# Cross-attention of 16 batches on one core: special keys' K kept on chip, another order of the first loads, first row maxima on ACT's queue, an end in two chains

## The chip, the core and the metric

The kernel runs on one core of a Trainium2 chip. A core has a matrix engine (TensorE, PE in the rows, with PEld for its weight loads), a vector engine (VectorE, DVE), an activation engine (ScalarE, ACT), a general engine (GpSimd, POOL) and a queue engine (SyncE, SP) that here only issues DMAs. ACT and POOL can issue DMAs as well. The metric is device time in microseconds (us), the median of several runs. Before: 520.08 us, median of 3 runs (519.92 to 520.15).

## What is computed

```python
B, S, D, C = 16, 256, 320, 512        # batches, queries, model and context width
HEADS, NUM_IP, NUM_DUMMY = 20, 4, 4   # head width 16; 256 keys per batch
text, ip_h = ctx[:, :248], ctx[:, 248:]
q = split_heads(x @ w_q)
out_text = softmax(q @ split_heads(text @ w_k).T / 4) @ split_heads(text @ w_v)
mask = ip_mask(bbox)                  # 0 or -10000 per query and special key
out_ip = softmax(q @ split_heads(ip_h @ w_k_ip).T / 4 + mask) @ split_heads(ip_h @ w_v_ip)
out = (merge(out_text) + merge(out_ip)) @ w_out + b_out + x
```

248 of the 256 keys of a batch are text keys. The last 8 are the special keys; their K and V come from other weights, and they have a softmax of their own.

## The kernel before, in words

**Arithmetic.** Every projection is done with split operands: ACT writes the rounded upper part of a matrix (`..._hi`), DVE the rest (`..._lo`), and PE sums three products (helper `three`, L659 to L661). x, ctx and the weights are split that way, and so is each K and Q tile on its way out of PSUM (ACT L461, then DVE L562, both into `qk_out`).

**Tiles.** Two batches form a group. A group has ten tiles: three K tiles (128, 128 and 64 rows by 512 columns), four V tiles (128 by 320), three Q tiles (like K). A K tile is twelve matmuls, so there are 24 K tiles with 288 matmuls in all. SP stores K and Q tiles to DRAM (`k_parts`, `q_parts`) and V tiles to `v_rows`, and reads them back in another layout into `k_stack`, `q_stack` (L280, L274, L276) and `v_stage` (L296). The stacks hold, per pair of heads, the upper and lower parts, mask rows, and a row of negative maxima. The K of the special keys of all batches is made once, in `special()`, split into `ksp_parts`, and POOL writes it into the last 8 columns of every batch in `k_parts` with six DMAs (L399). `load_stack_k(0)` waits for these six (`ksp_stored`).

**Lone tiles.** Tiles 0 to 14 run before any attention work. Tiles of later groups are hosted: PE does one after every second pair of heads (`tile` in the PE batch loop). ACT and DVE give a tile's PSUM bank free when they have read it; tile 15, the first hosted one, goes into the bank of tile 14.

**A batch.** `batch(t)` has ten steps p, one per pair of heads. PE computes the key-major scores of batch t (`key_scores`, L757, into `score_t`), the query-major scores of batch t + 1 (`query_scores`, L702), the products with V (`values`, L772), and the output projection of batch t - 1 (`project_out`, L781, into `pj`). ACT takes exp of the key-major scores (L503) and empties `pv` (L495). DVE takes row maxima of the query-major scores (L571, L573), turns them (`turn`, L579), and turns and inverts the results (L612, L615, L620). POOL normalises (L421, L426). The maxima go to DRAM (`store_rows`, L251) and back into the stack as a row (`load_rows`, L256), in two halves per batch; `key_scores` of a half waits for them. Batch -1 only makes maxima for batch 0, with tiles 15 to 19. DVE's `finish` (L627) adds the residual and SP stores the output (L303).

**Order.** All orders are written out by hand, one program per engine. SP runs its DMAs strictly in program order: an issue whose semaphore is late holds up all behind it. The same holds for ACT and DVE.

## Time and profile before

| what | value |
|---|---|
| median of 3 runs | 520.08 us |
| profiled execution, its own time | 520.33 us |
| its span | 518.5 us |
| PE busy | 477.4 us (92%) |
| DVE busy | 380.7 us (73%) |
| ACT busy | 275.3 us (53%) |
| POOL busy | 151.6 us (29%) |
| DMA moved | 101.80 MB, mean 196 GB/s |

The span is that of the recorded instructions; 1.83 us lie around it. Times below count from the start of the span. A row of a timeline gives start, duration, engine, line, operation, what is written from what is read, and in brackets the engine's idle time ahead of it with what ended it. Matmul durations overlap, so what one costs is the distance from start to start. A duration of a DMA on SPq is the issue alone, not the transfer.

### The profile page before, as it was taken

The page shows a single profiled execution, that of the slowest core. Times are in us where ns is not written, and L with a number is a line of the kernel's source. Part 1 is how long each engine was busy: PE and PEld are TensorE (multiplying, and loading weights), DVE is VectorE, ACT ScalarE, POOL GpSimd, SP SyncE. Part 2 cuts the span into 40 slices and gives each one's busy share as a digit, 9 for nine tenths or more (in the row PEclk, how much of TensorE's full clock was granted, in tenths as well). Part 3 has the DMA queues.
Part 4 walks back from the last instruction along what each step waited for, and adds up shares of the span by engine and source line. Part 5 has one row for each costly group of instructions (what it writes and reads, how often), then busy time and mean ns, then how long its engine had stood idle before and what let it go on. Part 6 is the DMA issues. An engine that isn't in the chain of part 4 may idle for free.

```text
span 518.5 us, 11114 instructions
## 1 busy us (share of the span) xinstructions
PE 477.4 (92%) x4306; PEld 321.8 (62%) x4306; DVE 380.7 (73%) x687; ACT 275.3 (53%) x355; POOL 151.6 (29%) x242
## 2 busy tenths in 40 slices
PE   2999669999999999999999999999999999898895
PEld 2787536576666766676666766676666765554542
DVE  3833476877877787877877787877887779999732
ACT  3643124465655656465655655465555546666670
POOL 4570000423313131414313141413304131543331
PEclk9999797999999999999999999999999999999998
DMA  8999975837593856837593856937584736273011
GB/s 272 303 232 290 351 255 163 261 107 231 150 326 100 282 179 166 278 114 246 149 332 96 268 194 170 274 111 246 148 284 149 256 123 210 86 252 84 9 53 51
DMA packets 96438, 101.80 MB, mean 196 GB/s; under 512 B 16881, under 2 KB 83489, under 8 KB 96385
## 3 DMA queue, kind: packets, MB, share of 16 engines
q1 hardware_dynamic: 95392, 98.92, 61.1%
q0 software_dynamic: 992, 2.17, 1.8%
q8 instruction: 34, 0.56, 0.4%
q14 instruction: 20, 0.16, 0.1%
HBM read 67.87 MB, written 33.23 MB: 195 GB/s over the span
## 4 chain that ended last, share of the span: by engine, by line
issue 54%; POOL 23%; PE 9%; DMA 5%; DVE 4%; SPq 2%; ACT 1%; POOLq 0%; ACTq 0%
POOL o_turned L421 10%; POOL o_all L426 6%; POOL x_all L413 5%; POOL v_cur L408 2%; DMA v_rows<-v_out 1%; PE score_q L659 1%; DMA q_parts<-qk_out 1%; PE pv L772 1%; PE score_q L660 1%; PE score_q L661 1%; DMA max_rows<-row_buf 1%; DMA probs<-in_wk 1%; PE pj L781 1%; DMA raw<-in_ctxT 1%; SPq L247 1%
## 5 line engine op out<-in xcount | busy, mean ns | idle before, releaser
L571 DVE TENSOR_REDUCE max_cols<-score_q 128x4 fp32r<-128x992 f32 x155 | 183.0, 1181 | 85.3 <-PE score_q L702 84.8
L503 ACT ACTIVATE probs<-score_t 128x1024 f32<-128x1024 f32 x160 | 163.4, 1021 | 145.5 <-PE score_t L757 145.5
L772 PE MATMUL pv<-probs,v_cur 128*32 128x256 f32 x1920 | 120.2, 383 | 0.6 <-ACT probs L503 0.6
L421 POOL TENSOR_TENSOR o_turned<-o_turned,inv_cols 128x256 f32<-128x256 f32 x80 | 54.4, 679 | 157.0 <-DVE inv_cols L615 157.0
L772 PEld LDWEIGHTS pv<-probs,v_cur 128*32 128x32 f32 x1920 | 54.3, 109 | 39.1 <-issue 1.0
L781 PE MATMUL pj<-wo_sb,o_all 128*128 128x320 f32 x192 | 70.4, 477 | 8.9 <-DVE out_sb L627 4.8
L413 POOL TENSOR_TENSOR x_all<-x_all,bias_sb 128x640 f32<-128x640 f32 x16 | 25.2, 1575 | 150.0 <-DMA x_all<-in_x 150.0
L612 DVE STREAM_TRANSPOSE o_turned<-o_all 128x512 f32<-128x512 f32 x80 | 55.9, 698 | 11.9 <-ACT o_all L495 11.9
L757 PEld LDWEIGHTS score_t<-q_stack,k_stack 64*128 64x128 f32 x440 | 33.0, 185 | 48.5 <-issue 34.8
L495 ACT ACTIVATE o_all<-pv 128x512 f32<-128x512 f32 x80 | 47.8, 598 | 28.5 <-PE pv L772 28.5
L757 PE MATMUL score_t<-q_stack,k_stack 64*128 64x256 f32 x440 | 55.7, 331 | 7.6 <-ACT probs L503 6.9
L702 PE MATMUL score_q<-k_stack,q_stack 64*128 64x256 f32 x420 | 43.5, 285 | 7.7 <-DMA q_stack<-aux_rows 5.3
L781 PEld LDWEIGHTS pj<-wo_sb,o_all 128*128 128x128 f32 x192 | 31.9, 193 | 25.9 <-DVE out_sb L627 8.4
L659 PE MATMUL score_q<-wv_hl,c_hi 128*128 128x320 f32 x112 | 40.2, 359 | 0.0
L702 PEld LDWEIGHTS score_q<-k_stack,q_stack 64*128 64x128 f32 x420 | 32.9, 188 | 9.9 <-issue 7.2
L426 POOL TENSOR_TENSOR o_all<-o_turned 128x128 f32<-128x128 f32 x80 | 36.6, 457 | 6.3
L661 PE MATMUL score_q<-wv_hl,c_hi 128*128 128x320 f32 x112 | 35.3, 315 | 0.0
L660 PE MATMUL score_q<-wv_hl,c_lo 128*128 128x320 f32 x112 | 35.2, 315 | 0.0
L659 PE MATMUL score_q<-c_hi,wk_hl 128*128 128x512 f32 (+1 forms) x72 | 32.6, 452 | 0.0
L661 PE MATMUL score_q<-c_lo,wk_hl 128*128 128x512 f32 (+1 forms) x72 | 29.1, 404 | 0.0
L660 PE MATMUL score_q<-c_hi,wk_hl 128*128 128x512 f32 (+1 forms) x72 | 29.0, 403 | 0.0
L562 DVE TENSOR_TENSOR qk_out<-score_q,qk_out 128x512 fp32r<-128x512 f32 (+1 forms) x40 | 27.4, 685 | 1.7 <-ACT qk_out L461 1.3
(151 smaller groups left out, 656.0 us busy)
## 6 DMA issues: line engine op xcount, KB each, us to landing
k_stack<-k_parts SPq DMA_DIRECT2D x33, 320.0 KB, 4.9
q_stack<-q_parts SPq DMA_DIRECT2D x33, 320.0 KB, 5.7
q_parts<-qk_out SPq DMA_DIRECT2D x32, 256.0 KB, 4.7
k_parts<-qk_out SPq DMA_DIRECT2D x32, 248.0 KB, 5.3
raw<-in_ctxT SPq DMA_DIRECT2D x14, 512.0 KB, 4.4
v_rows<-v_out SPq DMA_DIRECT2D x32, 160.0 KB, 4.7
v_stage<-v_rows SPq DMA_DIRECT2D x16, 320.0 KB, 6.2
x_all<-in_x SPq DMA_DIRECT2D x16, 320.0 KB, 6.1
```

Source lines behind the costliest of these rows:

```text
L421: pool.tensor_tensor(out, out, inv_cols[:, n % SLOTS, :].unsqueeze(2).broadcast_to([P, 2 * S // 32, DH]), ALU.mult).then_inc(scaled, 1)
L426: pool.tensor_tensor(o_norm_t[:, k // 2, :, half:half + DH], out[:, 0:S // 32, :], out[:, S // 32:, :], ALU.add).then_inc(o_added, 1)
L503: nc.scalar.activation(probs[:, slot(t % 2, p), :], score_t[:, :], ACT.Exp, scale=SCALE)\
L571: nc.vector.tensor_reduce(out=max_cols[:, h, :, at:at + 4:2].rearrange("p t e -> p e t"), in_=both[:, :, :, 0:TEXT], op=ALU.max, axis=AX.X ...
L612: nc.vector.transpose(turned_blocks(n), o_raw[:, n % SLOTS, :].rearrange("p (j n) -> p j n", n=32))\
L659: mm(out, w_hi, x_hi_, start=start, stop=False)
L660: mm(out, w_lo, x_hi_, start=False, stop=False)
L661: return mm(out, w_hi, x_lo_, start=False, stop=stop)
L702: last = mm(score_bank(b, p, e)[:, tile * KEYS:(tile + 1) * KEYS], q_cols(b % 3, p, e, tile * P, P), k_cols(b % 3, p, e, 0, KEYS), start=T ...
L757: last = mm(score_t[:, 512 * e + S * tile:512 * e + S * tile + S], k_cols(b % 3, p, e, tile * P, P), q_cols(b % 3, p, e, 0, S), start=True ...
L772: last = mm(pv[32 * t:32 * t + 32, at:at + S], values_of(u, kind, 4 * k + t), probs[:, slot(u, 2 * k + t // 2), a:a + S], start=kind != 1, ...
L781: last = mm(pj[:, 0:D], o_norm[:, b % 2, c, t * P:t * P + P], wo_sb[:, c, :], start=c == 0, stop=c == OC - 1)
```

## The change

The K columns of the special keys no longer go through DRAM on their own. `ksp_parts` has its own memory and stays. A K tile is now computed, split and read out in its text columns only (2 x 248 instead of 512, helper `columns`). Then DVE copies the special columns of the group from `ksp_parts` into `qk_out` (`fill`), and SP stores whole rows after `k_filled`. For tiles 0 to 2 the fill comes after `special()`; POOL's six DMAs and `ksp_stored` are gone.

SP's first loads and stores are reordered. The V tiles 3 and 4 and the c loads of group 1 go ahead of the stores of K tiles 0 to 2, `load_stack_k(0)` ahead of the Q stores, `load_x(1)` behind `load_stack_q(0)`, `load_small` into batch 0. ACT and DVE split x of group 1 later. The first half of the first row maxima is stored and loaded by ACT. `turn` stands directly behind its last maxima.

In the last batch the odd steps of `key_scores` use a second bank, and `project_out` of the last batch runs both row tiles side by side in two banks, each with its own store.

The diff, cut to its core:

```diff
@@ tiles and banks @@
+        ksp_parts = sb("ksp_parts", [P, 2, XC, P], f32r)
-        ksp_parts = o_turned[:, 0:2 * XC * P].bitcast(f32r).rearrange("p (s m n) -> p s m n", s=2, m=XC)
+        def key_bank(b, p):
+            return score_q[:, 0:1024] if b == B - 1 and p % 2 else score_t[:, :]
+        def out_bank(b, t):
+            return score_t[:, 0:D] if b == B - 1 and t else pj[:, 0:D]
+        def columns(row, j):
+            return row if j >= 3 else row.rearrange("p (b n) -> p b n", b=GB)[:, :, 0:TEXT]
@@ SP @@
-                sp.wait_ge(lo_done, 6 * g + j + 1)
+                if j >= 3:
+                    sp.wait_ge(lo_done, 6 * g + j + 1)
+                else:
+                    sp.wait_ge(k_filled, 3 * g + j + 1)
                 for s in range(2):
...
+                    parts = q_parts if j >= 3 else k_parts
+                    sp.dma_start(parts[s, m * P:m * P + r, g * GT:(g + 1) * GT], src[:, s, :])\
+                        .then_inc(qk_stored[ring], 16)
...
-            lone(0, 5)
+            lone(3, 5)
             for h in range(2):
                 load_c(1, h)
+            lone(0, 3)
             lone(5, 7)
-            load_x(1)
+            load_stack_k(0)
             lone(7, 10)
-            sp.wait_ge(ksp_stored, 96)
-            load_stack_k(0)
             sp.wait_ge(aux_stored, 96)
             load_stack_q(0)
-            lone(10, 12)
+            load_x(1)
+            lone(10, 14)
             sp.wait_ge(sp_stored, 16)
-            load_small()
-            lone(12, 14)
...
-                if host and t % 2 and g + 1 < GROUPS:
+                if host and t > 0 and t % 2 and g + 1 < GROUPS:
                     load_c(g + 1, 0)
                 if ahead:
                     need(sp, st_ready, PAIRS * t)
                     load_stack_k(t + 2)
+                if t == -1:
+                    load_c(g + 1, 0)
...
-                if next_:
+                if next_ and t >= 0:
                     store_rows(t + 1, 0)
...
-                if next_:
+                if next_ and t >= 0:
                     load_rows(t + 1, 0)
@@ POOL @@
-            for m, r in enumerate(MT_ROWS):
-                pool.wait_ge(ksp_lo, m + 1)
-                for s in range(2):
-                    pool.dma_start(k_parts[s, m * P:m * P + r, :].rearrange("p (b n) -> p b n", b=B)[:, :, TEXT:KEYS],
-                                   ksp_parts[0:r, s, m, :].rearrange("p (b n) -> p b n", b=B).bitcast(f32))\
-                        .then_inc(ksp_stored, 16)
@@ ACT @@
-            tile(10)
+            for n in range(10, 14):
+                tile(n)
             split_x(1)
-            for n in range(11, 14):
-                tile(n)
+            def store_first_rows():
+                act.wait_ge(rows_turned, 1)
+                act.dma_start(max_rows[0].rearrange("r (t i n) -> i r t n", t=2, i=4),
+                              row_buf[:, 0, :].rearrange("p (t n) -> p t n", t=2)).then_inc(first_stored, 16)
+            def load_first_rows():
+                act.wait_ge(first_stored, 16)
...
+                    if t == -1 and p == 6:
+                        store_first_rows()
+                    if t == -1 and p == 8:
+                        load_first_rows()
@@ DVE @@
+                if j < 3 and g:
+                    fill(g, j)
+            def fill(g, m):
+                r, w = MT_ROWS[m], GB * NSP
+                nc.vector.tensor_copy(
+                    qk_out[0:r, m, :, :].rearrange("p s (b n) -> p s b n", b=GB)[:, :, :, TEXT:KEYS],
+                    ksp_parts[0:r, :, m, g * w:(g + 1) * w].rearrange("p s (b n) -> p s b n", b=GB))\
+                    .then_inc(k_filled, 1)
...
-            tile(10)
+            for n in range(10, 13):
+                tile(n)
             split_x(1)
-            tile(11)
-            tile(12)
@@ PE @@
-                need(pe, exp_done, PAIRS * b + p)
+                if b < B - 1 or p == 0:
+                    need(pe, exp_done, PAIRS * b + p)
+                elif p == 1:
+                    pe.wait_ge(max_done, PAIRS * B)
+                else:
+                    pe.wait_ge(exp_done, PAIRS * b + p - 1)
...
+LAST_OUT = {3: [(0, 0), (1, 0), (0, 1), (1, 1)], 5: [(0, 2), (1, 2)]}
```

SP's queue from the stores of K tile 2 (before) to the mask row of the first stack. Before:

```order
L247 DMA k_parts<-qk_out 64x2x248 x2
L233 DMA v_rows<-v_out 128x320 x2
L217 DMA raw<-in_ctxT 128x2x512
L217 DMA o_all<-in_ctxT 128x2x512
L233 DMA v_rows<-v_out 128x320 x2
L224 DMA o_all<-in_xT 128x2x512
L226 DMA o_all<-in_xT 64x512 x2
L242 DMA q_parts<-qk_out 128x512 x4
L242 DMA q_parts<-qk_out 64x512 x2
L280 DMA k_stack<-k_parts 32x10x256 x3
L274 DMA q_stack<-q_parts 32x10x256 x3
L276 DMA q_stack<-aux_rows 32x10x256
```

Now, from the c loads to the x load:

```order
L223 DMA raw<-in_ctxT 128x2x512
L223 DMA o_all<-in_ctxT 128x2x512
L251 DMA k_parts<-qk_out 128x512 x4
L251 DMA k_parts<-qk_out 64x512 x2
L239 DMA v_rows<-v_out 128x320 x2
L284 DMA k_stack<-k_parts 32x10x256 x3
L251 DMA q_parts<-qk_out 128x512 x4
L251 DMA q_parts<-qk_out 64x512 x2
L278 DMA q_stack<-q_parts 32x10x256 x3
L280 DMA q_stack<-aux_rows 32x10x256
L230 DMA o_all<-in_xT 128x2x512
L232 DMA o_all<-in_xT 64x512 x2
```

The K stores moved behind the c loads, the K reads moved ahead of the Q stores, and the x load moved from ahead of the Q stores to behind the mask row.

ACT's queue from tile 10 to the first exp. Before (v_out rows are V tiles 13 to 16, x_hi the split of x of group 1, c_hi the two halves of c of group 2):

```order
L461 ACTIVATE qk_out<-pj 128x512
L445 ACTIVATE x_hi<-o_all 128x1536
L461 ACTIVATE qk_out<-pv 128x512
L461 ACTIVATE qk_out<-score_t 64x512
L456 ACTIVATE v_out<-score_t 128x320
L454 ACTIVATE v_out<-score_q,text_mask 128x320
L456 ACTIVATE v_out<-score_q 128x320
L454 ACTIVATE v_out<-score_q,text_mask 128x320
L441 ACTIVATE c_hi<-raw 128x1024
L461 ACTIVATE qk_out<-score_q 128x512 x2
L441 ACTIVATE c_hi<-raw 128x1024
L503 ACTIVATE probs<-score_t 128x1024
```

Now, from tile 13:

```order
L459 ACTIVATE v_out<-score_t 128x320
L448 ACTIVATE x_hi<-o_all 128x1536
L457 ACTIVATE v_out<-score_q,text_mask 128x320
L459 ACTIVATE v_out<-score_q 128x320
L457 ACTIVATE v_out<-score_q,text_mask 128x320
L444 ACTIVATE c_hi<-raw 128x1024
L464 ACTIVATE qk_out<-score_q 128x512
L496 DMA max_rows<-row_buf 4x64x32
L464 ACTIVATE qk_out<-score_q 128x512
L444 ACTIVATE c_hi<-raw 128x1024
L501 DMA q_stack<-max_rows 4x5x256
L515 ACTIVATE probs<-score_t 128x1024
```

The split of x moved behind tiles 11 to 13 and stands directly ahead of tile 14; two DMAs of the row maxima joined the queue, the second behind the second half of c.

PE at the very end, from the last key-major scores (with waits). Before:

```order
L757 MATMUL score_t<-q_stack,k_stack 128x256 [waits exp_done]
L757 MATMUL score_t<-q_stack,k_stack 128x256 x3
L781 MATMUL pj<-wo_sb,o_all 128x320
L772 MATMUL pv<-probs,v_cur 32x256 [waits exp_done,o_evac]
L772 MATMUL pv<-probs,v_cur 32x256 x11
L781 MATMUL pj<-wo_sb,o_all 128x320 [waits out_done,o_ready]
L781 MATMUL pj<-wo_sb,o_all 128x320 [waits o_ready] x2
L781 MATMUL pj<-wo_sb,o_all 128x320 [waits out_done]
L781 MATMUL pj<-wo_sb,o_all 128x320 x2
```

Now:

```order
L790 MATMUL score_q<-q_stack,k_stack 128x256 [waits exp_done]
L790 MATMUL score_q<-q_stack,k_stack 128x256 x3
L814 MATMUL pj<-wo_sb,o_all 128x320
L805 MATMUL pv<-probs,v_cur 32x256 [waits exp_done,o_evac]
L805 MATMUL pv<-probs,v_cur 32x256 x11
L814 MATMUL pj<-wo_sb,o_all 128x320 [waits out_done,o_ready]
L814 MATMUL score_t<-wo_sb,o_all 128x320 [waits out_done]
L814 MATMUL pj<-wo_sb,o_all 128x320 [waits o_ready]
L814 MATMUL score_t<-wo_sb,o_all 128x320
L814 MATMUL pj<-wo_sb,o_all 128x320 [waits o_ready]
L814 MATMUL score_t<-wo_sb,o_all 128x320
```

The three matmuls of the second row tile moved from behind the first tile's `finish` to between the first tile's own, in a bank of their own, and the last key scores are in `score_q`.

## Rows read from the trace of the kernel before

**Rows 1.** Page, part 1: busy time of each engine.
```profile
PE 477.4 (92%) x4306; PEld 321.8 (62%) x4306; DVE 380.7 (73%) x687; ACT 275.3 (53%) x355; POOL 151.6 (29%) x242
```

**Rows 2.** Matmul groups, 100 to 430 us: busy, mean ns, idle before, what ended it.
```profile
L781 PE MATMUL pj<-wo_sb,o_all 128*128 128x320 f32 x132 | 47.3, 467 | 6.1 <-DVE out_sb L627 4.2 <-DVE o_all L620 1.9
```

**Rows 3.** Stretches: length, PE, PEld, DVE, ACT, POOL busy, clock, DMA share, GB/s.
```profile
34.00:36.00 2.00, 2.00 (x10) 1.64 (x9) 1.18 (x2) 2.00 (x3) 2.00 (x3) 1.00 0.97 108
```

**Rows 4.** SP's issues, timeline; SPq L247 and L242 merge six issues with waits between.
```profile
15.61 7.98 SPq L247 DMA_DIRECT2D k_parts<-qk_out  x6
...
37.81 6.15 SPq L242 DMA_DIRECT2D q_parts<-qk_out  x6
44.22 1.98 SPq L280 DMA_DIRECT2D k_stack<-k_parts  x3
47.38 1.90 SPq L274 DMA_DIRECT2D q_stack<-q_parts  x3
```

**Rows 5.** Four K stores issued from 50.0 to 51.8 us: issue to landing.
```profile
DMA to landing us min/median/max: 5.2/5.9/6.7
```

**Rows 6.** DVE's timeline, the start.
```profile
28.27 0.28 DVE L597 TENSOR_TENSOR o_turned<-score_q,o_turned 64x128 fp32r<-64x128 f32 x1 [0.42 <-ACT o_turned L478]
...
47.52 1.22 DVE L551 TENSOR_TENSOR x_lo<-o_all,x_hi 128x1024 fp32r<-128x1024 f32 x1 [0.69 <-ACT x_hi L445]
48.78 0.69 DVE L553 TENSOR_TENSOR x_hi<-o_all,x_hi 64x512 fp32r<-64x512 f32 x1
...
68.71 1.27 DVE L547 TENSOR_TENSOR c_lo<-raw,c_hi 128x1024 fp32r<-128x1024 f32 x1
```

**Rows 7.** PE's timeline, the start; the times in brackets are idle time.
```profile
55.95 0.80 PE L702 MATMUL score_q<-k_stack,q_stack 64*128 64x256 f32 x4 [5.32 <-DMA q_stack<-aux_rows]
...
57.10 0.63 PE L659 MATMUL score_q<-wv_hl,c_hi 128*128 128x320 f32 x1
...
60.60 0.70 PE L702 MATMUL score_q<-k_stack,q_stack 64*128 64x256 f32 x4
...
80.42 0.79 PE L659 MATMUL score_q<-c_hi,wk_hl 128*128 128x512 f32 x1
```

**Rows 8.** The chain that ended last, 44 to 80 us: start, duration, what.
```profile
46.01 1.49 ACT x_hi L445
...
66.31 4.75 DMA max_rows<-row_buf
...
71.69 4.28 DMA raw<-in_ctxT
...
76.00 1.06 ACT c_hi L441
```

**Rows 9.** PE's timeline: where a 512-column tile and two 320-column tiles start.
```profile
17.51 0.40 PE L659 MATMUL score_t<-c_hi,wk_hl 128*64 128x512 f32 x1
...
20.27 0.30 PE L659 MATMUL score_t<-wv_hl,c_hi 128*128 128x320 f32 x1
...
22.03 0.31 PE L659 MATMUL score_q<-wv_hl,c_hi 128*128 128x320 f32 x1
```

**Rows 10.** Timeline of all engines: the last batch and the end.
```profile
495.08 1.50 PE L772 MATMUL pv<-probs,v_cur 128*32 128x256 f32 x24
...
498.21 0.50 PE L757 MATMUL score_t<-q_stack,k_stack 64*128 64x256 f32 x4 [0.46 <-ACT probs L503]
...
498.65 1.50 PE L772 MATMUL pv<-probs,v_cur 128*32 128x256 f32 x24
...
510.40 0.81 PE L781 MATMUL pj<-wo_sb,o_all 128*128 128x320 f32 x2 [0.61 <-DVE o_all L620]
511.24 0.49 DVE L627 TENSOR_TENSOR out_sb<-pj,x_all 128x320 f32<-128x320 f32 x1 [0.90 <-PE pj L781]
...
515.81 0.38 SPq L303 DMA_DIRECT2D out<-out_sb  x1
```

**Rows 11.** The last output store, issued at 515.81 us: issue to landing.
```profile
DMA to landing us min/median/max: 2.3/2.3/2.3
```

More of the change, by code:

```diff
@@ L360, in _ @@
                 batch(t)
-            for b in (B - 2, B - 1):
-                store_out(b)
-            sp.wait_ge(out_stored, 16 * B)
+            store_out(B - 2)
+            for t in range(OT):
+                sp.wait_ge(out_done, OT * (B - 1) + t + 1)
+                at = (B - 1) * S + t * P
+                sp.dma_start(out[at:at + P, :], out_sb[:, t, :]).then_inc(out_stored, 16)
+            sp.wait_ge(out_stored, 16 * (B - 1 + OT))
         @block.gpsimd
@@ L460, in tile @@
                     need(act, qk_stored[j % 3], 32 * (2 * g + j // 3))
-                    nc.scalar.activation(qk_out[0:r, j % 3, 0, :], tile_bank(n)[0:r, :], ACT.Copy).then_inc(hi_done, 1)
+                    nc.scalar.activation(columns(qk_out[0:r, j % 3, 0, :], j), columns(tile_bank(n)[0:r, :], j),
+                                         ACT.Copy).then_inc(hi_done, 1)
             high(wk_hl[:, 0], wk_raw, ld["wk"], 16)
@@ L577, in turn @@
                 dve.wait_ge(max_done, PAIRS * b + HALF * (h + 1))
-                need(dve, rows_stored, 16 * (2 * b + h - 1))
+                if b == 1 and h == 0:
+                    dve.wait_ge(first_stored, 16)
+                need(dve, rows_stored, 16 * (2 * b + h - 2))
                 nc.vector.transpose(row_buf[:, h, :].rearrange("p (t n) -> p t n", t=2),
@@ L626, in finish @@
                     dve.wait_ge(biased, b + 1)
-                nc.vector.tensor_tensor(out_sb[:, t, :], pj[:, 0:D], x_res[:, b % 2, t, :], ALU.add)\
+                nc.vector.tensor_tensor(out_sb[:, t, :], out_bank(b, t), x_res[:, b % 2, t, :], ALU.add)\
                     .then_inc(out_done, 1)
@@ L633, in batch @@
                         maxima(t + 1, p)
+                    if p % HALF == HALF - 1 and there(t + 1):
+                        turn(t + 1, p // HALF)
                     n = tile_due(t, p) if t >= 0 or p else None
@@ L649, in batch @@
                         split_x(g)
-                    if p % HALF == HALF - 1 and there(t + 1):
-                        turn(t + 1, p // HALF)
             for t in range(-1, B + 1):
@@ L666, in k_tile @@
                         pe.wait_ge(c_split, 2 * g + c // 2 + 1)
-                    last = three(out[0:r, :], wk_hl[:, 0, c, cols], wk_hl[:, 1, c, cols], c_hi[:, c, :],
-                                 c_lo[:, c, :], c == 0, c == CC - 1)
+                    last = three(columns(out[0:r, :], m), wk_hl[:, 0, c, cols], wk_hl[:, 1, c, cols],
+                                 columns(c_hi[:, c, :], m), columns(c_lo[:, c, :], m), c == 0, c == CC - 1)
                 last.then_inc(tile_ready, 1)
@@ L753, in key_scores @@
                     pe.wait_ge(rows_loaded[p // HALF], 16 * (b + 1))
-                need(pe, exp_done, PAIRS * b + p)
+                if b < B - 1 or p == 0:
[4 more added lines that the diff above has]
+                    pe.wait_ge(exp_done, PAIRS * b + p - 1)
+                both = key_bank(b, p)
                 for tile in range(2):
                     for e in range(2):
-                        last = mm(score_t[:, 512 * e + S * tile:512 * e + S * tile + S],
+                        last = mm(both[:, 512 * e + S * tile:512 * e + S * tile + S],
                                   k_cols(b % 3, p, e, tile * P, P), q_cols(b % 3, p, e, 0, S), start=True, stop=True)
@@ L779, in project_out @@
                 if c == 0:
-                    need(pe, out_done, OT * b + t)
-                last = mm(pj[:, 0:D], o_norm[:, b % 2, c, t * P:t * P + P], wo_sb[:, c, :],
+                    need(pe, out_done, OT * b + (t if b < B - 1 else 0))
+                last = mm(out_bank(b, t), o_norm[:, b % 2, c, t * P:t * P + P], wo_sb[:, c, :],
                           start=c == 0, stop=c == OC - 1)
@@ L785, in batch @@
             def batch(t):
+                if t == 1:
+                    pe.wait_ge(ld["small"], 32)
                 if t == 0:
-                    pe.wait_ge(ld["small"], 32)
                     for back in range(1, 6):
@@ L798, in batch @@
                             values(t + off, k)
-                    for m, k in OUT.get(p, ()):
+                    for m, k in (OUT if t < B else LAST_OUT).get(p, ()):
                         if there(t - 1):
```

29 lines of the change are left out of this document (14 added, 15 removed).

## The prediction

> **What bounds the kernel now.** I read the page's busy shares first: PE is busy for 92% of the span [rows 1], so a microsecond counts only where PE is shortened or stops waiting. The matmul groups of 100 to 430 us then show where it waits inside the regular batches: one group has idle time ahead of it, 6.1 us in 330 [rows 2]. There PE is the bound, and DVE, ACT, POOL or DMA work that changes is free. What is left is the start and the end. At the start PE idles 5.32 us ahead of the first query scores, until the mask row (aux_rows) of the first stack has landed [rows 7]; SP's issues and the chain of waits say what holds that up and what follows [rows 4, 8]. At the end the timeline shows PE, ACT and DVE taking turns [rows 10].
>
> **Regular batches.** A 512-column tile starts 2.76 us ahead of the next tile and a 320-column one 1.76 us, twelve matmuls each [rows 9]: 0.230 and 0.147 us a matmul, 0.43 ns a column. Sixteen columns fewer are 6.9 ns. 18 of the 24 K tiles are hosted, 216 matmuls, so 1.5 us go. The six lone tiles lose 0.5 us, which only lengthens the wait for the stack. That the operand is now two pieces of 248 columns is in no row; I take it as free, with the price in a rival below. DVE gains 24 small copies, near 0.2 us each (the nearest row is the 64x128 subtraction, 0.28 [rows 6]). They stand behind the subtraction that frees the PSUM bank, so PE doesn't wait for them; only SP's K store does. **-1.5 us**, between -1.5 and 0.
>
> **Start, the first stack.** What goes are POOL's six DMAs of 32-byte pieces; in 34 to 36 us the DMA engines were 97% busy for only 108 GB/s [rows 3]. What is added is a wait: the stores of K tiles 0 to 2 were issued from 15.6 to 23.6 us [rows 4] and now need the special keys' K, whose last lower part is done at 28.55 [rows 6]. With the copy they are issued until about 30.4. They land behind c and the POOL loads; the landings of 5.2 to 6.7 us in a full queue [rows 5] make it 35.6 to 37.1, I take 36. On SP the reads of K stand behind that wait, and behind them the Q stores: 36 + 2.0 for three reads [rows 4] + six issues at 0.65 (a third of 1.98) = 41.9, against 43.96 before (37.81 + 6.15). The Q stack reads were issued 3.4 us behind that end (47.38), so now at 45.3. From there to PE's start it took 8.57 us (55.95 - 47.38), so PE starts at about 53.9, 2.1 us earlier. The bounds are 0.5 (K stores land last) and 4 us (the queue is empty).
>
> **Start, what comes next.** The x load of group 1 was ahead of the Q stores; now it stands behind the mask row. Four issues of 0.65 put it at 47.9 to 49.8. The K stores that stood in that place took 5.2 to 6.7 us [rows 5], so x is in at about 55.2. On ACT the split of x (1.49, [rows 8]) now stands directly ahead of V tile 14, and tile 15 needs that tile's PSUM bank: 55.2 + 1.5 + 0.45 for the eviction = 57.2. Before, tile 15 started at 57.10 [rows 7]. On DVE the two subtractions, 1.22 + 0.69 [rows 6], stand ahead of the first maxima: these start at 58.6, and the next query scores, which need them, at 59.8. Before, these started at 60.60 and were held by tile 15, since PE ran at half its clock (tile 15 took 3.5 us where a V tile takes 1.76 [rows 7, 9]). So the 2.1 us are given back: behind tile 15 both kernels stand at the same point. I expect half clock there again, since PE has idled longer in pieces.
>
> **Start, the first row maxima.** Before, their store took 4.75 us to land, SP stood still for it, and the second half of c for group 2 went out behind it, at 71.69 [rows 8]. DVE had made room for it at 69.98 (68.71 + 1.27, [rows 6]). Now nothing blocks SP there, and c goes out 1.7 us earlier: 70.0, landing after 4.28 at 74.3, split by ACT until 75.4. But the load of the maxima stands behind that split on ACT. Issued at 75.4 it needs the 2.3 us of a small transfer without a queue [rows 11] (4.75 in a full one, [rows 8]): 77.7. Key scores of batch 0, exp (1.0), second key and query scores: the first hosted K tile starts near 79.9, against 80.42 [rows 7]. **-0.5 us** for the whole start. Its bounds are -4 (x and c land in time for PE to run through) and +3 (x lands 2 us late and half clock lasts longer).
>
> Here a rule of the Trainium skill speaks against the move. DMA: Bandwidth & Descriptors, section Issuing engines are not separate DMA queues, says that issuing from another engine saves only the issue time on the sequencer. By that rule the gain would be some 1.1 us of SP's two issues. The chain of waits of this case shows more: what SP loses is its standstill. By the rule alone the start would come out 0.6 us slower than I say.
>
> The small weights now load in batch 0, behind the residual; POOL's first normalisation waits for them about 1.3 us longer (two issues). Its first results are needed at the end of batch 0: nothing.
>
> **The last batch.** From one group of products with V to the next it takes 3.57 us (495.08 to 498.65). Of that 3.13 run over ACT's eviction and the odd step's exp to the even key scores at 498.21, and 0.44 are these key scores [rows 10]. With a second bank the key scores come earlier, and the period is 3.13, or PE's own work where two thirds of a projection stand in it (1.50 for the products, 2 x 0.44, and twice 0.54 = 3.46, less the overlap of their ends, about 3.4; 0.54 is an estimate from the 0.81 of a third's two matmuls, whose ends overlap what follows). The first group comes 0.44 earlier, the next three periods save 0.2, 0.44 and 0.2, the last 0.1. **-1.4 us**, between -0.6 and -2.
>
> **The end.** Before, the last third of the first row tile starts at 510.40 and its residual add at 511.24; only then the second row tile is multiplied, at half clock, and its store is issued at 515.81 [rows 10]. Now the second tile's third follows directly, 0.54 us later at full clock: result at 511.78, add until 512.3, store at 512.3. **-3.5 us**; -3.0 if PE is at half clock. The first tile's store is issued half a microsecond earlier and lies beside it. POOL, which makes the last values, keeps its distance: its operations depend on the same evictions.
>
> **Sum.** -1.5 - 0.5 - 1.4 - 3.5 = -6.9. The profiled execution took 520.33 us (span 518.5 and 1.83 around it), so 513.4 for it; the median lies 0.25 below, which gives 513.2.
>
> **Rivals.** (1) The start works: K stores land by 35, x by 53.5, and tile 15 follows the first query scores at once. Then the 2 us of the first wait stay, and half clock goes with them (1.7 us for tile 15): 509.8. For it: the small pieces are gone from the busiest stretch. Against: x goes out behind two more sets of transfers than before. (2) The start loses: x lands at 57 to 58 behind the stack, tile 15 starts at 59.5, and the load of the maxima adds to it: 515.8. For it: the landings of 6.7 us. (3) The end gives less: exp stays the bound in the last batch, because ACT's evictions wait as before, and only the two chains help: 514.6. (4) Slower: the two-piece operand costs PE time at every piece. It decides at 288 matmuls x 19 ns = 5.4 us, which eats all other gains; at 30 ns each it is 8.6 us and gives 523.3. The slowest rate seen, half clock, would be 0.2 us each. Against it: the score matmuls write and read blocks of 256 columns at full pace. (5) The change doesn't remove the wait: the mask row lands when it did, since the Q reads wait for the Q stores all the same. That is inside the forecast, whose start gives next to nothing.
>
> **Chances.** Forecast 0.45, its own range 512 to 514.3; (1) 0.2, (2) 0.2, (3) 0.1, (4) 0.03; 0.02 for no change through several small losses. The range leaves out (4), the zero and the outer edges of (1) and (2): 509.8 to 516.6. A measurement of this kernel can tell about 0.2%, 1.0 us, from no change. Faster 0.95, same 0.02, slower 0.03.
>
> **What would show it.** PE's idle time ahead of the first query scores: 3 to 4 us instead of 5.32. ACT's split of x: start at 55.2; the first hosted V tile right behind V tile 14's eviction. The load of the row maxima: issued behind ACT's second c split, near 75.4, with PE waiting for it at the first key scores. Matmuls of K tiles: start to start 0.223 us at full clock. Last batch: 3.13 to 3.4 us between groups of L772's kind. The last two stores of the output: about half a microsecond apart. I am wrong if K tile matmuls don't get shorter, if PE starts the first hosted K tile over 2 us off 79.9, or if the last two stores are over 1 us apart.

## The result: slower, not faster

The changed kernel took **523.13 us** (median of 13 runs, 521.37 to 527.66) against 520.08 of the kernel before (13 runs measured beside it, 517.17 to 521.85). The ratio is 1.0079 with a 95% interval of 1.0054 to 1.0105. The forecast was 513.2, its range ended at 516.6. So 10 us are missing, and the sign is wrong.

Lines of the profile's page of the kernel after, parts 1 and 5 (columns as in [rows 1]; in part 5 busy us and mean ns, then the idle time ahead of the group and what ended it):

```profile
span 521.7 us, 11133 instructions
PE 476.3 (91%) x4306; PEld 322.5 (62%) x4306; DVE 391.0 (75%) x711; ACT 275.2 (53%) x355; POOL 148.7 (29%) x236
...
L814 PE MATMUL pj<-wo_sb,o_all 128*128 128x320 f32 x186 | 66.9, 468 | 10.5 <-DVE out_sb L654 6.4
```

PE's work shrank by 1.1 us [rows 1], yet the span grew by 3.2. DVE has 10.3 us more: half of it (5.5) is the 24 small copies, nearly all of the rest one instruction that got longer, below. The matmul groups of 100 to 430 us show where PE stands still now. [Rows 2] had 6.1 us in one group; now it is 9.2 there and 2.5 ahead of the query scores (1.6 of it in the group shown):

```profile
L814 PE MATMUL pj<-wo_sb,o_all 128*128 128x320 f32 x130 | 46.5, 467 | 9.2 <-DVE out_sb L654 6.4 <-DVE o_all L647 2.8
...
L729 PE MATMUL score_q<-k_stack,q_stack 64*128 64x256 f32 x288 | 29.7, 283 | 1.6 <-DVE max_cols L597 1.5
```

To place the loss I compare the start of ACT's exp in both kernels. There is one for each step, ten for each batch, and I take the tenth of every batch as its end: the length of batch 2 runs from the last exp of batch 1 to the last exp of batch 2. Batch 2 (hosting, even) begins and ends so, first before, then after (where the last row is the end of batch 3):

```profile
133.77 1.02 ACT L503 ACTIVATE probs<-score_t 128x1024 f32<-128x1024 f32 x1
...
163.67 1.02 ACT L503 ACTIVATE probs<-score_t 128x1024 f32<-128x1024 f32 x1
```
```profile
135.23 1.02 ACT L515 ACTIVATE probs<-score_t 128x1024 f32<-128x1024 f32 x1
...
166.50 1.02 ACT L515 ACTIVATE probs<-score_t 128x1024 f32<-128x1024 f32 x1
...
194.98 1.02 ACT L515 ACTIVATE probs<-score_t 128x1024 f32<-128x1024 f32 x1
```

Batch 2 takes 29.90 us before and 31.27 after. Batch 3, odd, takes 28.48 in both (166.50 to 194.98; before 163.67 to 192.15). The same holds for batches 4, 6, 8 and 10. So the account by stages is: start +1.5 us (the lag at batch 2: 135.23 - 133.77), the ten batches 2 to 11 +6.6 together (all of it in the five even ones), last batches and end -4.9. The sum is +3.2. The end did what was forecast. The regular batches and the start did not.

The +1.5 flatters the start. The first exp comes 3.64 us later (80.60 against 76.96), and batch 0 gives 2.16 of that back (first exp to first exp 29.26 against 31.42). Some 1.2 of it is a long instruction that the kernel before has in batch 0 and the kernel after happens not to have, below.

### The profile page after: what moved, and what is told of

Read it like the earlier page. It is cut to its first block, busy times and chain, and to the rows that moved or that the text cites. A ratio compares the mean times of both kernels' runs of the same rounds, so it can differ in the third digit from the quotient of the medians.

```text
span 521.7 us, 11133 instructions
## 1 busy us (share of the span) xinstructions
PE 476.3 (91%) x4306; PEld 322.5 (62%) x4306; DVE 391.0 (75%) x711; ACT 275.2 (53%) x355; POOL 148.7 (29%) x236
## 4 chain that ended last, share of the span: by engine, by line
PE 62%; DVE 15%; issue 9%; DMA 7%; SPq 3%; POOL 2%; ACT 2%; POOLq 0%; DVEq 0%; ACTq 0%
PE pv L805 13%; PE score_t L790 9%; PE pj L814 9%; PE score_q L686 8%; PE score_q L688 7%; PE score_q L687 7%; PE score_q L729 5%; DVE max_cols L595 5%; DVE x_hi L569 2%; DVE qk_out L578 1%; DVE x_lo L567 1%; SPq L251 1%; DVE out_sb L654 1%; DMA o_all<-in_xT 1%; DMA k_parts<-qk_out 1%
## 5 line engine op out<-in xcount | busy, mean ns | idle before, releaser
L515 ACT ACTIVATE probs<-score_t 128x1024 f32<-128x1024 f32 x155 | 158.4, 1022 | 150.8 <-PE score_t L790 150.7
L424 POOL TENSOR_TENSOR o_turned<-o_turned,inv_cols 128x256 f32<-128x256 f32 x80 | 56.3, 704 | 171.8 <-DVE inv_cols L642 171.8
L814 PE MATMUL pj<-wo_sb,o_all 128*128 128x320 f32 x186 | 66.9, 468 | 10.5 <-DVE out_sb L654 6.4
L416 POOL TENSOR_TENSOR x_all<-x_all,bias_sb 128x640 f32<-128x640 f32 x16 | 27.1, 1696 | 137.7 <-DMA x_all<-in_x 110.1
L507 ACT ACTIVATE o_all<-pv 128x512 f32<-128x512 f32 x80 | 47.9, 599 | 32.2 <-PE pv L805 32.2
L790 PEld LDWEIGHTS score_t<-q_stack,k_stack 64*128 64x128 f32 x420 | 31.6, 186 | 45.3 <-issue 37.8
L790 PE MATMUL score_t<-q_stack,k_stack 64*128 64x256 f32 x420 | 53.2, 331 | 6.8 <-DMA q_stack<-max_rows 3.7
L814 PEld LDWEIGHTS pj<-wo_sb,o_all 128*128 128x128 f32 x186 | 30.0, 188 | 26.4 <-DVE out_sb L654 9.5
L686 PE MATMUL score_q<-c_hi,wk_hl 128*128 128x496 f32 (+1 forms) x72 | 32.1, 445 | 0.0
L687 PE MATMUL score_q<-c_hi,wk_hl 128*128 128x496 f32 (+1 forms) x72 | 28.8, 400 | 0.0
L688 PE MATMUL score_q<-c_lo,wk_hl 128*128 128x496 f32 (+1 forms) x72 | 28.7, 399 | 0.0
L597 DVE TENSOR_REDUCE max_cols<-score_q 128x4 fp32r<-128x32 f32 x155 | 28.0, 181 | 0.0
```

Source lines behind the costliest of these rows:

```text
L424: pool.tensor_tensor(out, out, inv_cols[:, n % SLOTS, :].unsqueeze(2).broadcast_to([P, 2 * S // 32, DH]), ALU.mult).then_inc(scaled, 1)
L507: nc.scalar.activation(o_raw[:, n % SLOTS, :], pv[:, :], ACT.Copy).then_inc(o_evac, 1)
L515: nc.scalar.activation(probs[:, slot(t % 2, p), :], key_bank(t, p), ACT.Exp, scale=SCALE)\
L686: mm(out, w_hi, x_hi_, start=start, stop=False)
L687: mm(out, w_lo, x_hi_, start=False, stop=False)
L688: return mm(out, w_hi, x_lo_, start=False, stop=stop)
```

## What is different in an even batch

DVE's timeline in step 4 of batch 2, before, then after:

```profile
151.06 1.18 DVE L551 TENSOR_TENSOR x_lo<-raw,x_hi 128x1024 fp32r<-128x1024 f32 x1
152.28 0.69 DVE L553 TENSOR_TENSOR x_hi<-raw,x_hi 64x512 fp32r<-64x512 f32 x1
153.00 0.25 DVE L579 STREAM_TRANSPOSE row_buf<-max_cols 128x64 f32<-128x64 f32 x1
```
```profile
151.54 0.24 DVE L605 STREAM_TRANSPOSE row_buf<-max_cols 128x64 f32<-128x64 f32 x1
...
152.27 0.16 DVE L585 CAST qk_out<-ksp_parts 128x32 fp32r<-128x32 f32 x1
...
152.71 1.18 DVE L567 TENSOR_TENSOR x_lo<-raw,x_hi 128x1024 fp32r<-128x1024 f32 x1
153.92 1.95 DVE L569 TENSOR_TENSOR x_hi<-raw,x_hi 64x512 fp32r<-64x512 f32 x1
```

The same subtraction of 64x512 takes 0.69 us before and 1.95 after. POOL's timeline of the same stretch, before and after:

```profile
152.94 1.57 POOL L413 TENSOR_TENSOR x_all<-x_all,bias_sb 128x640 f32<-128x640 f32 x1 [10.92 <-DMA x_all<-in_x]
```
```profile
153.44 1.88 POOL L416 TENSOR_TENSOR x_all<-x_all,bias_sb 128x640 f32<-128x640 f32 x1 [9.83 <-DMA x_all<-in_x]
155.28 1.07 POOL L424 TENSOR_TENSOR o_turned<-o_turned,inv_cols 128x256 f32<-128x256 f32 x1
```

POOL adds the bias to the residual as soon as the residual has landed. Before, it begins 0.03 us ahead of the end of x_hi. After, it is asked for during x_lo, stands until that ends (1.88 instead of 1.57 us), and then x_hi, which also reads two operands from SBUF, stands until POOL's addition ends at 155.32; it ends at 155.87, 0.55 us later. POOL's next operation in turn takes 1.07 us, where it takes 0.62 before, since x_hi now stands in its way. It looks as if one of the two engines has to wait for the end of the other's whole operation. (Spans on POOL are rough in this profile; the reading rests on DVE's own row.) How this reaches PE is seen in its idle times in batch 2, before and then after:

```profile
151.19 0.81 PE L781 MATMUL pj<-wo_sb,o_all 128*128 128x320 f32 x2 [0.34 <-DVE o_all L620]
...
157.91 1.34 PE L781 MATMUL pj<-wo_sb,o_all 128*128 128x320 f32 x4 [0.36 <-DVE out_sb L627]
```
```profile
152.83 0.81 PE L814 MATMUL pj<-wo_sb,o_all 128*128 128x320 f32 x2 [0.56 <-DVE o_all L647]
...
157.24 0.51 PE L729 MATMUL score_q<-k_stack,q_stack 64*128 64x256 f32 x4 [0.45 <-DVE max_cols L597]
...
160.71 1.34 PE L814 MATMUL pj<-wo_sb,o_all 128*128 128x320 f32 x4 [0.81 <-DVE out_sb L654]
```

Behind x_hi, PE stands 0.45 us for the row maxima and 0.45 more for the output addition. The 0.22 more for o_all come ahead of x_hi, where the early turn and the new copy stand on DVE.

All instances of x_lo and x_hi from 90 to 400 us (minimum/median/maximum in ns), after and then before:

```profile
L567 DVE TENSOR_TENSOR x_lo<-raw,x_hi x6: 1180/1182/1214, 96.7 to 391.8; 128x1024 fp32r<-128x1024 f32 x6
L569 DVE TENSOR_TENSOR x_hi<-raw,x_hi x6: 690/1946/2066, 98.0 to 393.0; 64x512 fp32r<-64x512 f32 x6
```
```profile
L553 DVE TENSOR_TENSOR x_hi<-raw,x_hi x6: 689/690/1950, 95.2 to 386.0; 64x512 fp32r<-64x512 f32 x6
```

The kernel before has one of them too, in batch 0: its 1950. A mean hides it, the maximum shows it.

The Trainium skill has the rule: SBUF — State Buffer, section Who interferes with whom, says that a DVE tensor_tensor with both inputs in SBUF contends with GpSimd's reads. It calls the ports that the two share an exclusive lock, and says of DVE's two-port modes that the one issued first keeps them for its whole instruction while the other blocks fully. If that goes for tensor_tensor too, x_hi ends at POOL's end plus about its own time; the trace agrees (155.32 + 0.55, where x_hi alone takes 0.69).

## Experiments

Theory A: this exclusion costs the even batches 1.2 us each. Theory B: the K tiles' two-piece operand or the new copies do. For the start: the late x costs it, or the late first stack does. The first four kernels below ran on one chip, the next four (before_end, before_end_late, after_old_late, after_x_first) on a second, after_k3 and the three of x_first_k3 on a third. Each group had the kernel before beside it (519.82, 520.82 and 519.32 us); the ratios are to that, and kernels of different chips are best compared by them.

**POOL waits for the split of x (after_gate, before_gate).**

```diff
                 pool.wait_ge(xr_loaded[u], 8 * (b - u) + 16)
+                if hosted(b) and b % 2 == 0:
+                    pool.wait_ge(x_tail, (b + 4) // 2 + 1)
```

> The kernel after with one wait more: in the even hosted batches POOL's addition of bias to the residual starts only when DVE's second lower part of x is written. Theory A (DVE and POOL exclude each other on operations that read both operands from SBUF): the subtraction with output x_hi, 1.94 to 2.07 us in five batches, takes 0.69 in all of them, each of these batches gets about 1.3 us shorter, and the time falls by 6 to 6.7 us, from 523.1 to about 516.8. Theory B (the K tiles' two-piece operand and the added DVE copies cost the time): nothing changes, 523.1, or a little more, since POOL starts its normalisation up to 1 us later.

> The kernel before with the same wait on POOL. Its trace has one long x_hi subtraction (1.95 us, in batch 0) and margins of 0.6 to 1.7 us in the others. Theory A: 1.2 us go with the one of batch 0, 520.1 to about 518.9, and the spread between executions gets smaller, since no collision is left to chance. Theory B: no change, 520.1.

Measured: after_gate 519.58 us, ratio to before 0.9992 (0.9965 to 1.0020); before_gate 518.04, ratio 0.9958 (0.9929 to 0.9987). In both x_hi takes 0.69 us in every batch. Before_gate does what A said for the time, with 1.8 instead of 1.2 us by the medians and 1.2 in batch 0 of its trace. It didn't do what I expected for the spread: its 12 runs lie between 515.88 and 520.84, the 29 of the kernel before between 516.59 and 524.10. After_gate wins 3.5 us by the medians and 4.5 by the ratios, where 6 to 6.7 were expected. In its profiled execution the five even batches give back 4.4 us, and the start is 2.0 us later before the edit can act; such differences of 1 to 2 us in the start came between executions more than once, and I have no cause for them. Batch 2 fell from 31.27 to 30.58 only: POOL's results now come later, and the third small copy of the batch still meets POOL's copy of V, as in the kernel after (0.43 us, 0.16 alone). So B falls, but a wait is a poor cure.

**The turn of the maxima alone (after_turn_old, before_turn_new).** In after_turn_old the turn goes back behind the split, in before_turn_new it comes ahead. The edit of before_turn_new (that of after_turn_old is its reverse):

```diff
                     if there(t + 1):
                         maxima(t + 1, p)
+                    if p % HALF == HALF - 1 and there(t + 1):
+                        turn(t + 1, p // HALF)
...
-                    if p % HALF == HALF - 1 and there(t + 1):
-                        turn(t + 1, p // HALF)
```

> The kernel after with DVE's turn of the row maxima back at the end of its step, behind the split of x. The split moves 0.25 us forward. Theory A with the phase as cause: POOL's addition still starts ahead of x_hi by 0.1 to 0.6 us in four of the five batches, so only one or two collisions go: 1.3 to 2.7 us less, about 521. Rival (the place of the turn by itself makes the loss): all of it goes, 516.5 to 517.

> The kernel before with only the turn of the maxima moved ahead of the hosted tile. The split of x moves back by 0.25 us, the margin to POOL's addition shrinks from 0.6 or more to 0.35 or more. Theory A with the phase as cause: no new collision, 520 within 1 us. Rival (the place of the turn by itself): five collisions of 1.3 us, 526.5.

Measured: after_turn_old 517.59 us, ratio 0.9956 (0.9929 to 0.9983); before_turn_new 526.09 (four runs), ratio 1.0102 (1.0059 to 1.0144). Here the rival's numbers came out, not mine. The mechanism was still the collision. In after_turn_old every x_hi takes 0.69 us. In before_turn_new, where nothing but this line is changed, one of the two is long in each of the five batches (four times x_hi, once x_lo):

```profile
L551 DVE TENSOR_TENSOR x_lo<-raw,x_hi x5: 1180/1184/2487, 151.3 to 389.9; 128x1024 fp32r<-128x1024 f32 x5
L553 DVE TENSOR_TENSOR x_hi<-raw,x_hi x5: 999/1950/1959, 152.5 to 391.1; 64x512 fp32r<-64x512 f32 x5
```

I had moved only DVE's side of the race by 0.25 us. The turn also releases SP's store of the maxima, and all of SP's later issues stand behind that store. SP's timeline from the last store of batch 3 to the residual of batch 4, before and before_turn_new:

```profile
194.94 0.54 SPq L251 DMA_DIRECT2D max_rows<-row_buf  x1
...
205.22 0.47 SPq L300 DMA_DIRECT2D x_all<-in_x  x1
```
```profile
194.17 0.54 SPq L251 DMA_DIRECT2D max_rows<-row_buf  x1
...
205.28 0.47 SPq L300 DMA_DIRECT2D x_all<-in_x  x1
```

By batch 4 before_turn_new lags by 1.09 us in exp, yet it stores the maxima 0.77 us earlier and issues the residual at the same time: 1 us earlier in its own step. In batch 2, where there is no lag yet, the residual goes out 0.42 us earlier (146.06 against 146.48). So the split comes later and the residual earlier. Both push towards the collision.

**POOL's addition moved away (before_end_late, after_old_late, after_x_first, after_k3).** Before_end takes only the change's end over into the kernel before (key_bank, out_bank, the waits of the last batch's key scores, LAST_OUT and the two stores):

```diff
-                    for m, k in OUT.get(p, ()):
+                    for m, k in (OUT if t < B else LAST_OUT).get(p, ()):
...
-            for b in (B - 2, B - 1):
-                store_out(b)
+            store_out(B - 2)
+            for t in range(OT):
+                sp.wait_ge(out_done, OT * (B - 1) + t + 1)
...
```

Before_end_late also moves the addition:

```diff
...
+                late = hosted(b) and b % 2 == 0
+                if not late:
+                    add_bias()
                 for k in range(QUADS):
+                    if k == 2 and late:
+                        add_bias()
```

> The kernel before with only the end of the change: a second bank for the odd key scores of the last batch, its output as two chains in two banks, two stores. Theory A (the end works and lies on its own): the last exp 0.7 us earlier and 4.0 us less from there to the last store, as the trace of after shows, 520.1 to about 515.4. Rival (part of the 4 us comes from the later phase of the kernel after): 517 or more.

> The same, and in the even hosted batches POOL's addition of bias to the residual moved behind its second group of products (k = 1), where DVE has no subtraction from SBUF. Theory A (exclusion of DVE and POOL): the long x_hi of batch 0 goes, 1.3 us less than before_end, 514.1, and five executions in a row lie closer together. Theory B (the long x_hi is hidden or due to something else): the same as before_end.

Measured: before_end 515.82 us (514.60 to 516.81), ratio 0.9905 (0.9875 to 0.9936); before_end_late 514.24 (513.95 to 514.49), ratio 0.9878 (0.9849 to 0.9906). The end is worth 5 us on its own. The collision of batch 0 costs 1.6 by the medians and 1.2 at the first exp of batch 1 in the traces (its x_hi: 1.95, then 0.69), and the spread shrinks from 2.2 to 0.5 us, over six and five runs. That the order of two engines, set by when a DMA lands, is behind a part of the spread of the kernel before is possible but not shown: before_gate still ranged over 5.0 us, and no collisions were counted run by run.

> The kernel after with the turn of the maxima at its old place and POOL's addition moved as in before_end_late. Theory A: x_hi takes 0.69 us in every batch, and POOL doesn't wait as it did in after_gate: no batch is longer than in the kernel before. Start 1.5 to 2.5 us later than before, last batch and end 4.7 earlier, K tiles up to 0.8 us: 516.5 to 517.5.

(The kernel is after_turn_old with POOL's addition moved as in before_end_late.) Measured: 520.87 us, ratio 1.0013 (0.9993 to 1.0033), 3.4 above the upper end of what I expected; by the ratios 3.0 more than after_turn_old. I had removed one collision and made another. DVE's and POOL's timelines of this kernel:

```profile
158.96 0.79 DVE L591 CAST qk_out<-ksp_parts 64x32 fp32r<-64x32 f32 x1
```
```profile
158.16 1.54 POOL L417 TENSOR_TENSOR x_all<-x_all,bias_sb 128x640 f32<-128x640 f32 x1
```

The copy of 64x32 into the K tile, 0.16 us elsewhere, ends at 159.75, just behind POOL's addition (159.70). Its longest took 1.165 us. In before_end_late these copies don't exist, and the same place costs nothing (even batches 29.91 us). So a small copy between SBUF tensors is a victim as well, and it stands ahead of the output addition for which PE waits.

> The kernel after with one edit: in the even hosted batches POOL adds the bias behind its third group (ahead of k = 3), where DVE has neither the split of x nor the small copy into a K tile. The turn stays ahead. Theory A (exclusion): x_hi takes 0.69 us in all batches, no batch gets longer than in the kernel before, 6.3 us less than after: 516.8. Rival (the early turn costs the time in itself, as before_turn_new's 6.3 us may be read): 522 to 523.

Edit: `k == 3` in place of `k == 2`, in the kernel after. Measured: 517.97 us (517.05 to 519.92), ratio 0.9965 (0.9941 to 0.9989): by the medians 5.2 less than after, by the ratios 5.9. x_hi takes 689 to 690 ns in all batches:

```profile
L575 DVE TENSOR_TENSOR x_hi<-raw,x_hi x6: 689/689/690, 98.0 to 388.3; 64x512 fp32r<-64x512 f32 x6
```

So one moved instruction of an engine that is 29% busy turns the change from slower to faster.

**The start (after_x_first).** On after_old_late:

```diff
             lone(5, 7)
+            load_x(1)
             load_stack_k(0)
             lone(7, 10)
             sp.wait_ge(aux_stored, 96)
             load_stack_q(0)
-            load_x(1)
```

(and split_x(1) behind tile(10) on ACT and DVE again).

> after_old_late with the load of x for group 1 ahead of the first stack's reads and of the Q stores, and its split at its old place behind tile 10, as before. Theory A (the late x is the loss of the start: x landed at 57.71, tile 15 at 59.69 against 57.10 in the kernel before): the start gets 2 us shorter than in after_old_late, 514.5 to 515.5. Rival (what x wins the stack loses, since its reads then land behind x): the first query scores start 1 us later and the time stays at that of after_old_late.

Measured: 517.27 us, ratio 0.9944 (0.9920 to 0.9969): 3.6 less than after_old_late; in the two traces the first exp of batch 1 comes 2.6 us earlier. (The 514.5 to 515.5 that I expected started from 517 for after_old_late.) PE's timeline at the start, after and then after_x_first:

```profile
54.66 0.80 PE L729 MATMUL score_q<-k_stack,q_stack 64*128 64x256 f32 x4 [4.54 <-DMA q_stack<-aux_rows]
55.22 0.66 PE L729 MATMUL score_t<-k_stack,q_stack 64*128 64x256 f32 x4
59.69 0.64 PE L686 MATMUL score_q<-wv_hl,c_hi 128*128 128x320 f32 x1 [3.81 <-ACT v_out L457]
```
```profile
56.24 0.80 PE L737 MATMUL score_q<-k_stack,q_stack 64*128 64x256 f32 x4 [5.83 <-DMA q_stack<-aux_rows]
...
57.39 0.63 PE L694 MATMUL score_q<-wv_hl,c_hi 128*128 128x320 f32 x1
```

The stack comes 1.6 us later with x ahead of it, and PE stands longer for it. But then nothing stands behind x: tile 15 starts at 57.39 instead of 59.69. The wait for x weighed more than the one that the change set out to remove.

**Put together (x_first_k3 and two variants).** x_first_k3 is after_x_first with the addition ahead of k = 3. The first variant leaves the turn ahead; the second takes the first maxima back to SP:

```diff
-                if next_ and t >= 0:
+                if next_:
                     store_rows(t + 1, 0)
...
-                    if t == -1 and p == 6:
-                        store_first_rows()
-                    if t == -1 and p == 8:
-                        load_first_rows()
```

> after_x_first with POOL's addition ahead of k = 3 instead of k = 2. In after_x_first the third small copy of each even hosted batch took 0.79 us until POOL's addition ended, and these batches were 0.6 us longer each. Theory A: this copy takes 0.17 to 0.43 us, 5 x 0.6 less, and of the K tiles' 16 columns 0.8 us are left over against before_end_late: 513.8. Rival (the copies cost these 0.6 us by themselves): 517.

> x_first_k3 with the turn of the maxima ahead of the hosted tile, as in after. Theory A: with no collision left to meet, the place of the turn is worth nothing or little either way, 513.8 within 0.7. Rival: 5.5 to 6.3 us more, 520.

> x_first_k3 with the first row maxima stored and loaded by SP's queue as in the kernel before. If moving them to ACT's queue gains what the prediction counted for it (the first hosted K tile at 79.9 instead of 80.42), this one is 0.5 us slower than x_first_k3; if their load stands longer behind ACT's work than it would on SP, it is 0.5 to 1.5 us faster.

Measured: x_first_k3 514.63 us (513.24 to 515.48), ratio 0.9891 (0.9853 to 0.9928); with the turn ahead 515.17, ratio 0.9900 (0.9863 to 0.9938); with the first maxima on SP again 513.64 (513.21 to 514.44), ratio 0.9876 (0.9836 to 0.9916).

With no collision of the split to meet, the early turn costs 0.5 us by the medians, which is within the spread of both, and 1.0 in the traces, about 0.25 in each even batch: it is most likely its own 0.25 us, ahead of operations for which PE waits. The rival's 5.5 us did not appear. The length of batch 2, from the last exp of batch 1 to its own last, in the traces (the third column for this batch alone):

| kernel | turn | long x_hi or copy | batch 2, us |
|---|---|---|---|
| before | late | no | 29.90 |
| before_turn_new | early | yes | 31.01 |
| after | early | yes | 31.27 |
| after_gate | early | copy 0.43 | 30.58 |
| after_k3 | early | no | 30.10 |
| after_turn_old | late | no | 29.83 |
| after_old_late | late | copy 0.79 | 30.35 |
| x_first_k3 | late | no | 29.83 |
| x_first_k3_turn_new | early | no | 30.11 |

So of the 1.37 us that after loses in an even batch some 0.2 are left with the early turn alone (30.10 against 29.90), and 1.17 are the collisions: that of x_hi, and that of the third small copy with POOL's copy of V (0.42 us), which after_k3 is rid of as well.

The maxima on ACT's queue cost 1.0 us more than on SP's by the medians. Six runs each overlap in their ranges, so this alone is at the edge of the noise; the traces place it, with the first exp 1.8 us later on ACT's queue and the last one 0.9. ACT's timeline of x_first_k3, and the chain of the variant on SP:

```profile
74.36 1.06 ACT L450 ACTIVATE c_hi<-raw 128x1024 fp32r<-128x1024 f32 x1 [4.21 <-DMA raw<-in_ctxT]
74.37 0.54 ACTq L508 DMA_DIRECT2D q_stack<-max_rows  x1
78.11 1.02 ACT L522 ACTIVATE probs<-score_t 128x1024 f32<-128x1024 f32 x1 [2.69 <-PE score_t L798]
```
```profile
66.47 3.89 DMA max_rows<-row_buf
...
70.38 0.56 SPq L260
...
70.98 4.37 DMA raw<-in_ctxT
```

On ACT the load stands in order behind the split of c, whose wait ends when c lands. On SP it goes out at 70.38, 4 us earlier. c lands 1.0 us later for it (75.35 against 74.33), but the first exp no longer waits for the maxima: it starts at 76.34 instead of 78.11.

Before_end_late (514.24) and x_first_k3_rows_sp (513.64) both beat the kernel before, by ratios of 0.9878 and 0.9876, and with it the kernel after. They ran on different chips, and I can't tell them apart. So what the special keys on chip add over the end and the moved addition is within the noise; the traces give 0.8 us at the last exp.

## Point by point: why the prediction was wrong

- **"There PE is the bound, and DVE, ACT, POOL or DMA work that changes is free": this step failed, for 6.6 us.** [Rows 2] spoke against it: the 6.1 us idle ahead of the output projection end with DVE's out_sb and o_all. PE is busy for 98% of that stretch (323.9 of 330 us; 92% is the whole span), and still waits for DVE once or twice a batch. What comes ahead of those operations on DVE isn't free. I asked what the small copies and the turn cost by their own time, and not which operation of POOL they would be moved beside. The trace of before had the sign of it, one x_hi of 1.95 us. In place of the free DVE and POOL work the runs showed 1.17 us in each even batch from collisions, x_hi's above all, and 0.2 us more in each even batch from the early turn: with the addition moved and nothing else (after_k3), the even batches take 30.1 instead of 31.3 us.
- **K tile matmuls: right in kind, half in size.** PE's timeline of a K tile after, twelve matmuls from the first row to the second:

```profile
38.29 0.39 PE L686 MATMUL pj<-c_hi,wk_hl 128*128 128x496 f32 x1
...
41.01 0.39 PE L686 MATMUL pv<-c_hi,wk_hl 128*128 128x496 f32 x1
```

  They stand 0.227 us apart, where 0.223 was forecast and 0.230 measured before [rows 9]. That is 0.7 us for 216 matmuls instead of 1.5. Of this the even batches keep about 0.05 each (before_end_late against x_first_k3); the rest may go to the copies on DVE, which no run shows. Rival (4), a dear two-piece operand, is out. (Its threshold counted 288 matmuls, though by the prediction's own account the 72 of the lone tiles aren't on the path.)
- **First stack: 1.3 of the forecast 2.1 us.** The last K store was issued at 31.44 (forecast until 30.4) and landed by 37.8, not 36, so the K reads and the Q stores behind them went out 1.9 us later than forecast, the Q stores from 39.95 to 44.32. The last of them landed 3.60 us after its issue at 43.73, and the Q reads went out at 47.41, not at 45.3. PE still started at 54.66 (forecast 53.9, before 55.95): the mask row landed 5.0 us after its issue, and from the Q reads to PE's start it took 7.25 us instead of 8.57. PE's idle time fell from 5.32 to 4.54, not to 3 or 4.
- **x of group 1: wrong by 2.5 us.** It went out at 50.07 to 51.79 instead of 47.9 to 49.8, and landed 6.44 us after the issue of its last piece, at 57.7. ACT's split started at 57.74 (forecast 55.2), tile 15 at 59.69 (57.2). This is rival (2) to within 0.2 us. It had a chance of 0.2, since I took the middle of the landings in [rows 5] where their upper end came. Half clock came there as forecast: the granted clock was 0.50 from 60 to 63 us (0.82 before), and tile 15 took 3.50 us again.
- **First row maxima: right mechanism, wrong account.** The load was issued by ACT at 76.96 (forecast 75.4), behind the second half of c, and the key scores waited 3.66 us for it. The second half of c went out at 72.64 (forecast 70.0), since the late start had moved all of this back. The first hosted K tile started at 82.92, not 79.9: over 2 us off, the sign that the prediction itself named for being wrong. I weighed SP's standstill and took ACT's queue as a given; the variant on SP shows the first exp 1.8 us earlier with them left there. The rule of the Trainium skill that the prediction draws on (DMA: Bandwidth & Descriptors, Issuing engines are not separate DMA queues) pointed the right way, since it grants only the issue time as gain; of the wait in order on ACT's queue, which made it a loss, it doesn't speak.
- **Last batch: half.** Forecast -1.4, measured -0.7. Where four matmuls of the projection stand in a period, it stays at 3.57 us (499.03 to 502.60; before, 498.65 to 502.22), against a forecast of 3.4. The others take 3.2 (495.81 to 499.03), where before one took 3.57 [rows 10] and the last already 3.2.
- **End: right.** PE's timeline and SP's stores after:

```profile
512.63 1.50 PE L805 MATMUL pv<-probs,v_cur 128*32 128x256 f32 x24 [0.56 <-ACT probs L515]
...
517.58 0.81 PE L814 MATMUL pj<-wo_sb,o_all 128*128 128x320 f32 x2
518.22 0.70 PE L814 MATMUL score_t<-wo_sb,o_all 128*128 128x320 f32 x2
...
518.94 0.88 SPq L371 DMA_DIRECT2D out<-out_sb  x2
```

  From the last products with V to the last store's issue it takes 6.9 us (512.63 to 519.5) against 10.4 (505.44 to 515.81, the store of [rows 10]): -3.5, as forecast. The stores are 0.5 us apart, the granted clock was 0.98 from 515 us on, and the smaller last store lands in 1.8 instead of 2.3 us [rows 11]. Together with the last batch -4.7 against a forecast of -4.9, and before_end measured 5.0 alone.

All in all the sum was -1.5 - 0.5 - 1.4 - 3.5 and came out as +6.6 in the batches, +1.5 at the start, and -4.9 for what follows batch 11, of which -0.7 in the last batch and -4.0 from its last exp on. The right end was no luck: before_end shows it alone. That the start lost only 1.5 was: without the long x_hi of the kernel before in batch 0 it would have been about 2.7.

The chance of 0.03 for slower was the gravest error. The forecast and its rivals varied terms that I had already listed; none was a collision that no part of the change names.

## What to carry to other kernels

Where DVE and POOL both work from SBUF, list for each moved DVE instruction which POOL instruction it will run beside, and look at the maximum of each group, not at its mean: one long instance in the old trace is the price of a collision that the new order may meet every time. An instruction that is free by its own duration isn't free if it shifts a race whose other side is a landing DMA. And of a wait that is removed ask which load paid for it: here x went to the back of the queue for the stack, and cost more than the stack had.

## What the hardware showed unexpectedly

- A DVE subtraction with both operands in SBUF (64x512, 0.69 us) took 1.94 to 2.07 us when it began during POOL's addition; one of 128x1024 took 2.49 instead of 1.18 (before_turn_new); a copy of 64x32 took up to 1.17 instead of 0.16 (after_old_late). Each ended 0.03 to 1.1 us behind POOL's operation. DVE operations with an operand in PSUM were not visibly lengthened: in after_old_late the one ahead of the long copy, 64x496, took 0.67 us beside the same addition, and the mean of that shape after is 0.656.
- In these rows whoever comes second waits for the end of the other's operation. POOL's addition took 1.88 instead of 1.57 us when it came during x_lo, and x_lo, which was first, kept its 1.18.
- The profile shows this as a longer busy time of the instruction (x_hi's row: 1.95 us and no brackets), not as idle time: no wait and no releaser names it.
